# Expert layers: the rows of three of eight experts return by an accumulating indirect DMA, the other five by one-hot products

## The reference, cut to what matters

```python
probs = softmax(xn @ gate_w.T)                  # per token over 8 experts
g, m = top_k(probs.transpose(0, 2, 1), 128)     # each expert takes its 128 best tokens of a batch
xin = xn[batch, m]                              # gather
h = gelu(einsum('nekd,edf->nekf', xin, w1))     # 128 -> 512
h = einsum('nekf,efd->nekd', h, w2)             # 512 -> 128
out = zeros.at[batch, m].add(g[..., None] * h)  # back to the tokens
x = x + 0.5 * out
```

## Time and profile before

| | |
|---|---|
| Runs | 1666.23, 1667.79 (median), 1670.37 us |
| The profiled execution's own time | 1667.2 us |
| Its span, first to last instruction | 1665.5 us |
| Mean granted TensorE clock over the span | 0.927 |
| Busy share of the span: PE, DVE, ACT, POOL | 87%, 76%, 70%, 47% |
| First expert layer: choosing, experts | 871 to 912 us, 912 to 1190 us |
| Second expert layer: choosing, experts | 1330 to 1369 us, 1369 to 1665.5 us |

### The profile page before, as it was taken

One profiled execution on the slowest core, in us unless ns is written; L12 is line 12 of the kernel. 1 busy time (PEld: TensorE's weight loads), 2 busy tenths in 40 slices (PEclk: granted clock), 3 DMA queues, 4 the chain that ended last, 5 costly groups with the idle time before them and its releaser, 6 DMA issues. The chain is left out here.

```text
span 1665.5 us, 40705 instructions
## 1 busy us (share of the span) xinstructions
PE 1446.4 (87%) x12722; PEld 1003.0 (60%) x12722; DVE 1267.3 (76%) x3158; ACT 1160.5 (70%) x2439; POOL 778.2 (47%) x1204
## 2 busy tenths in 40 slices
PE   5999679999999999989970999999878609999998
PEld 2554334445454544435550899999745408999997
DVE  6777478888888888657848677877778586778776
ACT  5888337777777787758842778787566407887785
POOL 4687724545454444434415666554022106665540
PEclk9999759999999999989975899999989658999999
DMA  5022201111111111001012111110001101111110
GB/s 156 29 83 85 86 13 46 41 42 44 42 43 41 45 40 45 5 1 38 26 48 94 40 38 38 32 30 24 1 26 39 38 3 40 51 50 50 49 36 25
DMA packets 84640, 70.92 MB, mean 43 GB/s; under 512 B 16752, under 2 KB 78000, under 8 KB 84528
## 3 DMA queue, kind: packets, MB, share of 16 engines
q1 hardware_dynamic: 76336, 52.62, 11.3%
q0 software_dynamic: 8192, 16.79, 3.8%
HBM read 46.81 MB, written 22.54 MB: 42 GB/s over the span
## 5 line engine op out<-in xcount | busy, mean ns | idle before, releaser
L1111 DVE TENSOR_REDUCE at_negmax<-at_s_ps 128x2 f32<-128x1024 f32 (+3 forms) x384 | 389.4, 1044 | 64.7 <-PE at_s_ps L888 57.4
L1017 ACT ACTIVATE at_p<-at_x_ps 128x512 f32<-128x512 f32 x640 | 355.3, 596 | 98.9 <-PE at_x_ps L900 92.4
L1335 POOL DMA_INDIRECT e_x_in<-xn,e_row_c x256 | 259.2, 1012 | 146.0 <-issue 75.7
L1072 POOL TENSOR_SCALAR_AFFINE_SELECT at_p<-at_p 128x256 f32<-128x256 f32 (+1 forms) x448 | 191.3, 441 | 243.8 <-ACT at_p L1017 243.7
L900 PE MATMUL at_x_ps<-qr,kr 50*128 50x512 bf16 (+3 forms) x1024 | 227.4, 305 | 18.6 <-ACT at_p L1017 10.9
L1458 DVE TENSOR_TENSOR e_hid_lo<-e_hid,e_hid_hi 128x512 fp32r<-128x512 f32 x256 | 177.3, 693 | 86.8 <-ACT e_hid_hi L1422 77.2
L883 PE MATMUL at_s_ps<-kr,qr 48*128 48x512 bf16 (+3 forms) x1024 | 188.3, 312 | 18.3 <-PEq L1679 11.9
L1421 ACT ACTIVATE e_hid<-e_h_ps 128x512 f32<-128x512 f32 x256 | 154.9, 605 | 43.0 <-PE e_h_ps L1363 37.8
L916 PE MATMUL at_o_ps<-at_p,at_va 128*32 128x512 f32 (+3 forms) x2048 | 179.8, 447 | 0.0
L900 PEld LDWEIGHTS at_x_ps<-qr,kr 50*128 50x128 bf16 x1024 | 66.6, 94 | 153.6 <-ACT at_p L1017 136.8
L1363 PE MATMUL e_h_ps<-e_x_hi,w_hi 128*128 128x256 f32 x512 | 156.5, 306 | 0.0
(11 more groups left out here) (210 smaller groups left out, 3392.5 us busy)
## 6 DMA issues: line engine op xcount, KB each, us to landing
qr<-q_parts SPq DMA_DIRECT2D x128, 48.0 KB
kr<-k_parts SPq DMA_DIRECT2D x128, 48.0 KB
xres<-in_x_dram SPq DMA_DIRECT2D x8, 512.0 KB, 8.2
qr<-q_parts SPq DMA_DIRECT2D x128, 32.0 KB
xn<-m_n_xhat SPq DMA_DIRECT2D x16, 256.0 KB
e_x_in<-xn,e_row_c POOLq DMA_INDIRECT x256
xn<-sc_n_xhat SPq DMA_DIRECT2D x16, 256.0 KB
out_dram<-xres SPq DMA_DIRECT2D x16, 256.0 KB
```

The lines of the kernel that those rows point to most:

```text
L1017: a.activation(p_sb[g % 2][:, i, :], x_ps[i % 2][:], ACT.Exp, scale=SCALE).then_inc(x_read, 1)
L1072: sel = gp.affine_select(out=part, in_=part, compare_op=ALU.is_ge, fill=0.0, base=0, pattern=[[0, n] for n in part.shape[1:-1]] + [[1, P]] ...
L1111: v.tensor_reduce(out, scored, AX.X, ALU.max, negate=True).then_inc(s_read, 1)
L1335: nc.gpsimd.indirect_dma_start(out=x_in[k][u][:], out_offset=None, in_=xn_dram, in_offset=bass.IndirectOffsetOnAxis(ap=row_c[k][:, u:u + 1 ...
```

## The change

Experts 0, 2 and 4 (`BY_DMA`) no longer pass through `give_back`, `one_hot` and ACT's `weigh`. DVE weighs their result into `y_row` with one operation per batch, and POOL adds these rows by two indirect DMAs with `compute_op=ALU.add` per expert into a table in HBM, one table for even and one for odd batches. The table starts as the residual: SP stores `xres` into it (`keep_rows`, 16 DMAs of 256 KB) behind the weight loads while the tokens are chosen. After a batch's last such addition SP loads the batch back over `xres`, and DVE waits for that (`reloaded`) before it adds `o_ps`. The additions of one batch wait for each other (`scattered`). POOL's program is written out without a loop: in each step q it gathers for slot q + 8 and, where expert q - 4 is one of the three, adds for it. `row_c` and its copies are gone; the DMAs read `rows` directly.

```diff
--- before.py
+++ after.py
@@ -1156,7 +1156,7 @@
                 schedule(dve, first, step, flush)
 
 
-def split_weights(nc, block, sb, sem, h, weights):
+def split_weights(nc, block, sb, sem, h, weights, keep_rows):
 
     raw = [sb(f"raw{j}", [P, E, F], F32) for j in range(len(weights))]
     loaded = [[sem(f"raw{j}{e}_in") for e in range(E)] for j in range(len(weights))]
@@ -1168,6 +1168,7 @@
     def _(sp):
         for x, hi, lo, w, into in tiles:
             sp.dma_start(x, w).then_inc(into, 16)
+        keep_rows(sp)
 
     @block.scalar
     def _(act):
@@ -1183,7 +1184,11 @@
         pool.wait_ge(lo_done, len(tiles))
 
 
-def choose_tokens(nc, sb, sem, h, probs, name, weights=None):
+BY_DMA = (0, 2, 4)
+BY_PE = tuple(k for k in range(E) if k not in BY_DMA)
+
+
+def choose_tokens(nc, sb, sem, h, probs, name, keep_rows, weights=None):
 
 
     local = sb(f"{name}_local", [K, NB * E], F32)
@@ -1202,7 +1207,11 @@
...
             if weights is not None:
-                split_weights(nc, block, t, sem, h, weights)
+                split_weights(nc, block, t, sem, h, weights, keep_rows)
+            else:
+                @block.sync
+                def _(sp):
+                    keep_rows(sp)
 
             @block.tensor
             def _(pe):
@@ -1242,7 +1251,7 @@
     return local, rows, weight
 
 
-def experts_layer(nc, sem, h, xres, xn_dram, probs, name, out, weights=None, next_norm=None):
+def experts_layer(nc, sem, h, xres, xn_dram, sum_dram, probs, name, out, weights=None, next_norm=None):
 
 
 
@@ -1257,8 +1266,16 @@
         ps = lambda n, s: tmp.enter_context(nc.psum_tensor(f"{name}_{n}_ps", s, F32))
         s = lambda n: sem(f"{name}_{n}")
         two = lambda n, sh, d=F32R: [t(f"{n}{j}", sh, d) for j in range(2)]
-        local, rows, weight = choose_tokens(nc, lambda n, sh, d: tmp.enter_context(nc.sbuf_tensor(n, sh, d)), sem, h, probs, name, weights)
-        row_c = [t(f"row_c{k}", [K, U], U32) for k in range(S)]
+        sums_set = s("sums_set")
+        of_batch = lambda n: sum_dram[n % U][n * T:(n + 1) * T, :].rearrange("(c p) d -> p c d", p=P)
+        in_chunks = lambda n: xres[:, n, :].rearrange("p (c d) -> p c d", c=C)
+
+        def keep_rows(sp):
+            for n in range(NB):
+                sp.dma_start(of_batch(n), in_chunks(n)).then_inc(sums_set, 16)
+
+        local, rows, weight = choose_tokens(nc, lambda n, sh, d: tmp.enter_context(nc.sbuf_tensor(n, sh, d)), sem, h, probs, name,
+                                            keep_rows, weights)
         loc_c, wgt_c = two("loc_c", [K, U], F32), two("wgt_c", [K, U], F32)
         x_in = [[t(f"x_in{k}{u}", [K, D], F32) for u in range(U)] for k in range(S)]
...
@@ -1266,19 +1283,21 @@
         hid_hi, hid_lo = two("hid_hi", [P, FC, N]), two("hid_lo", [P, FC, N])
         y_t = two("y_t", [D, N], F32)
         y_hi, y_lo = two("y_hi", [K, U, D]), two("y_lo", [K, U, D])
+        y_row = {k: t(f"y_row{k}", [K, U, D], F32) for k in BY_DMA}
         hot = two("hot", [K, U, T])
         acc_sb = [t(f"acc_sb{u}", [D, T], F32) for u in range(U)]
         t_ps, yt_ps, y_ps, o_ps = ps("t", [D, N]), ps("yt", [D, N]), ps("y", [K, U, D]), ps("o", [P, T])
         h_ps = [ps(f"h{j}", [P, HC, N]) for j in range(2)]
         acc = [ps(f"acc{u}", [D, T]) for u in range(U)]
         gathered = [[s(f"gathered{k}{u}") for u in range(U)] for k in range(S)]
-        rows_done, cols_done, hot_done = s("rows_done"), s("cols_done"), s("hot_done")
+        scattered = {k: [s(f"scattered{k}{u}") for u in range(U)] for k in BY_DMA}
+        reloaded = [s(f"reloaded{u}") for u in range(U)]
+        cols_done, hot_done = s("cols_done"), s("hot_done")
...
-        acc_read, o_full, x_added, stored, pool_turn = (
-            s("acc_read"), s("o_full"), s("x_added"), s("stored"), s("pool_turn"))
+        acc_read, o_full, x_added, stored = s("acc_read"), s("o_full"), s("x_added"), s("stored")
...
@@ -1322,23 +1341,35 @@
 
             @block.gpsimd
             def _(pool):
-                def gather(i):
-                    for k in range(S):
-
-                        after(pool, t_full, (i - 1) * S + k + 1)
-                        pool.sem_inc(pool_turn, 1)
-                        of_turn = rows[:, bass.ds(i * U * E, U * E)].rearrange("p (u e) -> p e u", u=U)
-                        nc.gpsimd.tensor_copy(row_c[k][:], of_turn[:, k]).then_inc(rows_done, 1)
-                        pool.wait_ge(rows_done, i * S + k + 1)
-                        pool.sem_inc(pool_turn, 1)
-                        for u in range(U):
-                            nc.gpsimd.indirect_dma_start(
-                                out=x_in[k][u][:], out_offset=None, in_=xn_dram,
-                                in_offset=bass.IndirectOffsetOnAxis(ap=row_c[k][:, u:u + 1], axis=0)).then_inc(gathered[k][u], 16)
-
-                gather(0)
-                with pool.Fori(0, TU - 1) as r:
-                    gather(r + 1)
+                def gather(i, k):
+                    after(pool, t_full, (i - 1) * S + k + 1)
+                    for u in range(U):
+                        at = (i * U + u) * E + k
+                        nc.gpsimd.indirect_dma_start(
+                            out=x_in[k][u][:], out_offset=None, in_=xn_dram,
+                            in_offset=bass.IndirectOffsetOnAxis(ap=rows[:, at:at + 1], axis=0)).then_inc(gathered[k][u], 16)
+
+                def scatter(i, k):
+                    pool.wait_ge(yl_done, i * S + k + 1)
+                    if (i, k) == (0, BY_DMA[0]):
+                        pool.wait_ge(sums_set, NB * 16)
+                    for u in range(U):
+                        if k != BY_DMA[0]:
+
+                            pool.wait_ge(scattered[BY_DMA[BY_DMA.index(k) - 1]][u], i * 16 + 16)
+                        at = (i * U + u) * E + k
+                        nc.gpsimd.indirect_dma_start(
+                            out=sum_dram[u], out_offset=bass.IndirectOffsetOnAxis(ap=rows[:, at:at + 1], axis=0),
+                            in_=y_row[k][:, u, :], in_offset=None, compute_op=ALU.add).then_inc(scattered[k][u], 16)
+
+                LAG = 4
+                for k in range(S):
+                    gather(0, k)
+                for q in range(TU * S + LAG):
+                    if q + S < TU * S:
+                        gather(q // S + 1, q % S)
+                    if q >= LAG and (q - LAG) % S in BY_DMA:
+                        scatter((q - LAG) // S, (q - LAG) % S)
                 if next_norm is not None:
                     next_norm.root(pool, 0)
 
@@ -1382,14 +1413,16 @@
                     mm.then_inc(y_full, 1)
 
                 def give_back(i, k, q):
+                    if k in BY_DMA:
+                        return
                     pe.wait_ge(yl_done, q + 1)
-                    pe.wait_ge(hot_done, q + 1)
-                    if k == 0:
+                    pe.wait_ge(hot_done, i * len(BY_PE) + BY_PE.index(k) + 1)
+                    if k == BY_PE[0]:
 
                         after(pe, acc_read, i * U)
                     for u in range(U):
-                        pe.matmul(acc[u][:], y_hi[k % 2][:, u, :], hot[k % 2][:, u, :], start=(k == 0), stop=False, skip_group_check=True)
-                        mm = pe.matmul(acc[u][:], y_lo[k % 2][:, u, :], hot[k % 2][:, u, :], start=False, stop=(k == S - 1),
+                        pe.matmul(acc[u][:], y_hi[k % 2][:, u, :], hot[k % 2][:, u, :], start=(k == BY_PE[0]), stop=False, skip_group_check=True)
+                        mm = pe.matmul(acc[u][:], y_lo[k % 2][:, u, :], hot[k % 2][:, u, :], start=False, stop=(k == BY_PE[-1]),
                                        skip_group_check=True)
                     mm.then_inc(returned, 1)
 
@@ -1437,7 +1472,7 @@
                     run(i, k, (0, split_x), (1, gelu), (2, copy_y), (3, weigh))
                     turn = turn_at(i, k, SUMS_AT)
                     if turn is not None:
-                        act.wait_ge(returned, turn * S + S)
+                        act.wait_ge(returned, turn * len(BY_PE) + len(BY_PE))
                         for u in range(U):
                             a.activation(acc_sb[u][:], acc[u][:], ACT.Copy).then_inc(acc_read, 1)
 
@@ -1465,13 +1500,24 @@
                         v.tensor_copy(dst[k % 2][:], of_turn[:, k]).then_inc(cols_done, 1)
 
                 def weigh(i, k, q):
-                    dve.wait_ge(yh_done, q + 1)
+                    if k in BY_DMA:
+                        dve.wait_ge(y_full, q + 1)
+                        dve.wait_ge(cols_done, q * 2 + 2)
+                        for u in range(U):
+
+                            after(dve, scattered[k][u], i * 16)
+                            y = v.tensor_scalar(y_row[k][:, u, :], y_ps[:, u, :], wgt_c[k % 2][:, u:u + 1], None, ALU.mult)
+                        y.then_inc(yl_done, 1)
+                        return
+                    dve.wait_ge(yh_done, i * len(BY_PE) + BY_PE.index(k) + 1)
```

(19 more changed lines are left out.)

## The result

The changed kernel takes 1654.62 us (median of four, 1651.08 to 1656.08) beside 1667.07 for the kernel before in the same job: ratio 0.992, interval 0.9905 to 0.9935. That is 12.5 us less where the forecast had 43 less. The profiled execution took 1653.33. A second finding came with the experiments: in two later jobs, on other chips, the same program takes 1714, longer than before.

What follows compares the result with a forecast made beforehand. PE was taken to bound the expert stages: 1667.2 us profiled, less 44.6 for PE's dropped `give_back` steps, less 2.8 at the start, plus 4 for the first turn's reload, made 1624. The range for 8 in 10 was 1614 to 1665.

Steps and rivals of the forecast that it cites:

- POOL's term: POOL's 16 gathers and 6 additions a turn, priced as gathers, take 29.0 us, 2.8 less than PE.
- d: What an addition costs POOL above a gather's 1.016 us; taken as below 0.47, up to which PE stays the bound.
- Rival A: POOL becomes the bound in the expert turns with d above 0.47: total 1578.8 + 96 d, 1646 at d = 0.7; chance 0.18.
- PE's term: In the expert stages, 48 `give_back` steps go from PE at 0.93 us each: 44.6 us less, turn 34.60 to 31.8.
- Satisfied waits free, gap 0.30: On POOL, satisfied waits cost nothing, 0.30 us between transfers; upper bound 0.81 before 13 DMAs, 6.6 us more a turn.
- Starting up: In each layer's first two slots, gather pairs come 0.70 us sooner without the copy: 2.8 us less in all.
- The rule on two-port operations: DVE one-hots lock POOL out of writing descriptors: 33.6 us a turn, total near 1652; left out of the sum.
- Landing: Time until an addition's rows are in memory: 3 to 6 us, with no waiting up to 7.9.
- rival B: Additions land slowly and POOL stands in `scattered` waits: slower than before, 1710 at a landing of 12 us; chance 0.15.
- First turn's reload: In each layer's first turn the batch is reloaded late and DVE waits: 2 us per layer, 4 in all.
- The drains (rival C): Late reloads at layer ends, or table stores delaying first gathers, cost up to 3 us each per layer: 1628 to 1636; chance 0.10.
- ACT, `keep_rows`: ACT's changed work in the short slots and the table's 16 stores while choosing: cost nothing, the stores at most 3 us.

Runs made afterwards that it cites:

- Jobs one to four: The first four jobs of follow-up runs, each on one chip beside the kernel before; the changed kernel unedited took 1714.06 in the second, 1714.14 in the third.
- the written-out program: The kernel before with only POOL's loop written out for all eight turns, copies of the row numbers kept: 1667.87 us, ratio 0.9998.
- the two loops: The changed kernel with POOL looping over pairs of turns, row numbers from two small tables copied each turn: three experts 1728.51 us, experts 0 and 2 1704.41.
- the pause in the first turn: Old row-number copy and wait in turn 0 only: kernel before with direct row numbers, no additions, 1704.24 us; changed kernel with one expert 1691.11, two 1687.5.
- the full pause: Old copy, wait and both increments: kernel before with direct row numbers, first two turns, 1668.44 us; changed kernel, every gather pair, one expert 1652.08, two 1683.11.

## Why the prediction was wrong

**The step that failed** is POOL's term: "The slowest gather makes d = 0.40, and I take 'below 0.47'." It is 0.70 by the means, and most of it is accumulation itself (medians: 1.625 us against 0.997 for the same rows merely written). With it POOL's turn is 33.5 us as measured, where 29.0 was summed and PE's 31.8 was to be the bound, and PE stands idle before `o_ps` for 24.2 us in place of 1.8. The slowest gather, 1.42, was no bound for an operation that no row showed. Rival A was the mechanism: its price, 1578.8 + 96 d, gives 1646 for the measured d, and 1656 when the gathers' mean of 1.055 instead of 1.016 is put in too (16 x 16 x 0.039 = 10). It had 0.18. I had written beside it that an added row needs a second source, and should have given it most of the chance: POOL's margin was 2.8 us in a turn of 31.8, and beyond it each 0.2 us in six instructions over sixteen turns is 20 us of the total.

By the count of read descriptors in the Trainium skill ("Collectives: The Full Stack", why ReduceScatter is half of AllGather) an addition would take half more, which was an estimate; the runs show 0.63 more on 0.997. The direction agrees, and the size was past the edge. That the second read is the reason is not shown.

- **PE's term** held: 0.22 and 1.16 us on either side, the `e_acc_ps` matmuls are 2 x 160 = 320, and one expert alone, where PE bounds, gave 16.1 us for 16 steps. With three it was paid out only until POOL's turn was met: 34.6 - 33.5 = 1.1 of the 2.8 us a turn.
- **Satisfied waits free, gap 0.30**: held for gathers and additions. None of the 13 gaps of 0.81 came.
- **Starting up**: counted from PE's end of the choosing stage, slot 4 starts 1.9 us sooner in the first layer (19.39 in place of 21.27) and 1.5 in the second (19.20 in place of 20.70), 3.4 together for the 2.8 taken.
- **The rule on two-port operations** (the Trainium skill, "SBUF — State Buffer", "Who interferes with whom"): the estimate by it was 33.6 us a turn, near 1652, and the measured turn is 33.5. That agreement is chance: the gathers' mean rose by 0.04 us only, where the rule made five of sixteen 0.91 longer, and the excess stands in the additions' rows, where rows that are merely written do not have it.
- **Landing**: 3.2 to 4.5 us, within the 3 to 6 taken; rival B is excluded. The reload of 256 KB lands in 3.1 where 4 was taken.
- **First turn's reload**: PE's wait for it was 2.08 and 4.55 us, 6.6 where 4 was taken. DVE's waiting for reloads, 25.5 us in one layer, goes on through the layer, not in its first turn only, because POOL never gets nearer.
- **The drains (rival C)**: at the end of the second layer PE waits 0.88 us before the last `o_ps`, and 0.87 before the change: no cost of a late reload.
- **ACT, `keep_rows`**: no cost seen; the first choosing stage lasts 41 us as before.

**What no step foresaw** is the effect of the chip. Jobs one to four ran on three chips; in two of these jobs, on two of the chips, the unedited kernel was run and took 1714, and in all four jobs every kernel with an unpaced series of gathers came out above its own sum, by some 35 to 130 us, and by 11 with four experts. In two other jobs it took 1654. That it is the chip and not something else about a job is argued only: one chip alone came twice, with the loss both times. The kernel before took 1665 to 1669 in every job. Shown: the loss goes with idle times of ScalarE, the longest with PE's result long there; it needs no additions (gathers alone), it is not the written-out program (1667.87), not the large table (the two loops), nor, where I looked in the unedited kernel's first layer, the loading of instructions; its place followed the unbroken series (the pause in the first turn); with two and more experts it also comes in the steady state, 2 to 3 us at a time and up to 4.8 without accumulation. Open: what holds ScalarE up, why the kernel without accumulation, with the least work for GpSimd of the three-expert ones, was the slowest of all (1755.89), why some chips have it, and whether the full pause cures it there, since the runs meant to show that fell on a chip without it. The one outward sign I found is that the changed kernels' pages name no landing time for the gathers in the jobs that have it, and name 2.6 us in those without it; the kept page of the kernel before names none either, so the sign is a weak one.

## What to carry to other kernels

Price an accumulating indirect transfer at 1.6 to 1.7 us of GpSimd per 128 rows, with 0.30 to the next, before moving work to it: one expert by it gives as much here as three, which fill GpSimd. An operation that the trace has never shown has no upper bound in the trace; put the likeliest outcome where the engine that takes it becomes the bound. And run the unedited kernel in the same job as its variants: this one gains 12 to 14 us in one job and loses 45 to 47 in another, while the kernel before shows nothing.

## What the runs showed that I had not expected

Accumulation costs GpSimd 0.63 us per 128 rows (1.625 - 0.997, medians) though its data path is fast enough to land in 3.5 us. A pause of 0.81 us between pairs of gathers, which looked like waste in the earlier trace rows, is what the kernel before, steady on every chip, has and the unsteady ones lack in part or whole; whether it is the reason is open. And one program, unchanged, took 1654 in two jobs and 1714 in two others, with the kernel before equal in all.
